# A one-core AdaLN block: x of all batches kept in SBUF, the maxima's two parts made by POOL, the first quad's parts moved SBUF to SBUF

## The chip, the cores and the metric

The kernel runs on one core of one Trainium2 chip. The metric is the time of one execution on the device in microseconds; the figure used is the median of the runs. The kernel before has a median of 712.5 us over three runs (710.43 to 712.85).

## What is computed

The block has eight batches of 512 tokens with 128 features, 16 heads of width 8. All of it is fp32 in the reference:

```
mod = (silu(c) @ wmod)                      # shifts sa, sb, scales ca, cb, gates ga, gb of each batch
h = layernorm(x) * (1 + ca) + sa
q, k, v = h @ w_qkv.T, by head              # logits = q k^T / sqrt(8)
l = logits - max(logits)
p = where(l >= 0, pos(l), 1 / (1 - l (1 - l/2 (1 - l/3))));  p /= sum(p)
x = x + ga * (p v @ w_out.T + b_out)
h = layernorm(x) * (1 + cb) + sb
x = x + gb * ffn(h)                         # 128 (and its negative) -> 512 -> 512 -> 128, weights +-1, relu
```

Since the maximum is subtracted, l is never above zero and only the reciprocal of the cubic is needed.

## The kernel before, in words

The unit of work is a group m: two blocks of 128 keys against the 512 queries of two heads, so that a tile is 128x2048 in two halves. There are 128 groups, 16 to a batch, and the program is written as steps s, one group each: batch b = s // 16, step n = s % 16. For a group, PE makes scores into the PSUM tile Z in two halves (L532), ACT squares each half with a shift (sq, L685), DVE makes the cubic from sq and Z (cub, L918, `cubic`), POOL squares the cubic (L1104, `square_of`), ACT takes the reciprocal root of that (prob, L696), and PE multiplies prob with the values (OP, L564). The ring of cubics has four places; prob of group s - 2 is made in step s.

Seven groups ahead (`AHEAD`), PE makes the logits into SA (L547) and DVE reduces them to their maxima (mx, L927, `maxima`, two of 1024 columns a step). Every fourth group, in steps 1, 5, 9 and 13, a quad is complete. Then `of_maxima` on DVE splits the negated maxima into a rounded part (L937) and the rest (L941), and transposes both into mp (L947). Eight small DMAs on SP lay mp as rows into QH (`rows_of_maxima`), where the scores' matmul subtracts the maximum as a product with rows of ones of KH. Q and K themselves are each kept as two rounded parts; `write_parts` writes them to HBM (parts_q, parts_k), `read_parts` brings a quad's rows into QL, KH and QH. This holds for the first quad too: its K parts are written and read back on ACT's queue, its Q parts on SP's.

Beside the groups run the products of the table MISC: hT, q, k, v for batch b + 1, x1 and the second norm's transposes h2T and the layer l0 for batch b - 1, layer l1 and y for batch b - 2. An entry names the step and the place (a, b, c, d) of PE's sequence in `pe_step`; ACT takes the result out of PSUM in the same step and place (`take`). They share one PSUM bank MB, so each waits until the one before was taken. FILL puts a matmul without use into steps of the batches 0 and 1.

The table AT gives the steps of the small work. For the norm of x, DVE does four bn_stats (st1, L964) and four bn_aggr (mv1, L970) in the steps 6 and 7 for batch b + 2, POOL makes the root (rs1, L1063 and L1065) and xn (L1108 to L1114) in the steps 9 and 10. x arrives by two loads a batch: xa for the norm, xb for the residual. For the norm of x1 it is st2, mv2 on DVE and rs2, x1n on POOL. POOL also keeps a copy x1k of x1 for the last sum (L1144). In the last batch (b = 7) st2 and mv2 stand at the end of step 8, after its maxima, and rs2 and x1n in step 9.

Ahead of the steps, and in the steps of batch -1, stand the set-up and the parts, logits and maxima of the first quads. The gates' rows are made by DVE (`dve_gates`). After the steps, `pe_tail` and its partners do x1, norm and feed-forward of batch 7.

## Time and profile before

| | |
|---|---|
| median of three runs | 712.5 us |
| the profiled execution, its own time | 711.12 us |
| its span in the profile | 709.3 us |
| busy share of DVE, PE, ACT, POOL | 92, 89, 83, 85% |
| mean granted clock of PE | 0.969 of full speed |

The span is what the profile covers; the execution's own time is 1.8 us longer. A busy share is a mean over the whole span, with a start of 43 us in which little is busy, seven batches that repeat, and an end with another order. So the windows of one stage and the timeline of its engines say more than the shares.

### The profile page before, as it was taken

To read this page: it belongs to the slowest core of one execution; us is meant where nothing else is said; L and a number is where in the kernel's file an instruction comes from. 1 tells how busy PE (TensorE), PEld (TensorE's weight loads), DVE (VectorE), ACT (ScalarE), POOL (GpSimd) and SP (SyncE) were. 2 spreads that over 40 slices of the span, in tenths; PEclk is the share of its full clock that TensorE was granted. 3 is DMA by queue.
4 is the path that set the end of the run, shared out by engine and by line. 5 is a ranking of instruction groups with operands and counts; after the bars stand their busy time and mean duration, and the time that the engine had idled before them with its cause. 6 is when DMAs were issued, how large, how long until landed. Compare 5 with 4: busy or idle time off the path is not lost.

```text
span 709.3 us, 9702 instructions
## 1 busy us (share of the span) xinstructions
PE 628.1 (89%) x3009; PEld 245.3 (35%) x3009; DVE 649.6 (92%) x807; ACT 587.7 (83%) x541; POOL 601.8 (85%) x414
## 2 busy tenths in 40 slices
PE   7486778777789999899989999999989999997898
PEld 5132222223222334233523343233423342334356
DVE  6989999999999999999999999999999999985843
ACT  2037788988899989998999989998999989987942
POOL 7229697898979999899989999899989998898740
PEclk9568999999999999999999999999999999998999
DMA  4524112241134114151135114331214113100100
GB/s 129 176 61 163 46 54 67 77 151 29 53 93 169 50 54 108 55 171 31 38 102 171 50 51 108 113 113 53 57 55 164 54 53 92 51 8 24 34 12 30
DMA packets 43719, 56.24 MB, mean 79 GB/s; under 512 B 11548, under 2 KB 27188, under 8 KB 43668
## 3 DMA queue, kind: packets, MB, share of 16 engines
q1 hardware_dynamic: 42606, 54.17, 25.7%
q10 hardware_dynamic: 1062, 1.45, 0.6%
q8 instruction: 24, 0.39, 0.2%
q14 instruction: 27, 0.22, 0.1%
HBM read 32.06 MB, written 18.89 MB: 72 GB/s over the span
## 4 chain that ended last, share of the span: by engine, by line
PE 45%; DVE 24%; ACT 15%; issue 13%; DMA 1%; ACTq 0%; POOL 0%; DVEq 0%; POOLq 0%
DVE cub L918 11%; DVE mx L927 10%; PE OP L564 10%; PE MB L486 9%; PE Z L532 7%; PE SA L547 7%; ACT sq L685 6%; ACT prob L696 5%; PE MB L476 2%; PE MB L499 2%; PE MB L583 1%; PE MB L454 1%; ACT hid L739 1%; DVE st L975 1%; ACT OT L747 1%
## 5 line engine op out<-in xcount | busy, mean ns | idle before, releaser
L1104 POOL TENSOR_TENSOR cub<-cub 128x2048 f32<-128x2048 f32 x128 | 460.5, 3603 | 48.3 <-DVE cub L918 48.0
L685 ACT ACTIVATE sq<-Z,shift 128x1024 f32<-128x1024 f32 x256 | 282.4, 1117 | 74.9 <-PE Z L532 73.0
L918 DVE SCALAR_TENSOR_TENSOR cub<-sq,Z 128x1024 f32<-128x1024 f32 x256 | 309.6, 1210 | 16.2 <-ACT sq L685 15.7
L927 DVE TENSOR_REDUCE mx<-SA 128x2 f32<-128x1024 f32 x248 | 301.7, 1216 | 11.0 <-PE SA L547 8.0
L696 ACT ACTIVATE prob<-cub 128x2048 f32<-128x2048 f32 x128 | 244.4, 1911 | 0.5 <-PE OP L564 0.5
L547 PE MATMUL SA<-KH,QL 64*128 64x512 f32 x496 | 121.5, 486 | 37.5 <-DVE mx L927 28.0
L532 PE MATMUL Z<-QH,KH 64*128 64x512 f32 x512 | 129.0, 500 | 17.3 <-DVE cub L918 17.0
L564 PE MATMUL OP<-prob,Vq 128*16 128x512 f32 x1024 | 135.2, 601 | 0.0
L532 PEld LDWEIGHTS Z<-QH,KH 64*128 64x128 f32 x512 | 48.3, 184 | 196.1 <-DVE cub L918 116.1
L486 PE MATMUL MB<-hid,W 128*128 128x512 f32 x192 | 108.0, 645 | 0.0
L547 PEld LDWEIGHTS SA<-KH,QL 64*128 64x128 f32 x496 | 47.3, 187 | 120.5 <-DVE mx L927 89.5
L476 PE MATMUL MB<-h2T,W 128*128 128x512 f32 x56 | 32.4, 661 | 7.0 <-ACT hid L739 4.7
L486 PEld LDWEIGHTS MB<-hid,W 128*128 128x128 f32 x192 | 28.6, 188 | 23.4 <-issue 23.4
L583 PE MATMUL MB<-W,ident 128*128 128x512 f32 x52 | 33.1, 721 | 0.6 <-ACT x L721 0.6
L564 PEld LDWEIGHTS OP<-prob,Vq 128*16 128x16 f32 x1024 | 16.9, 94 | 45.6 <-issue 40.9
L499 PE MATMUL MB<-W2G,hid 128*128 128x128 f32 x192 | 29.0, 298 | 0.7 <-ACT x L721 0.7
L499 PEld LDWEIGHTS MB<-W2G,hid 128*128 128x128 f32 x192 | 24.6, 201 | 6.4 <-issue 5.5
L454 PE MATMUL MB<-hT,wq 128*128 128x512 f32 x16 | 10.7, 754 | 7.1 <-ACT hT L707 7.1
L747 ACT ACTIVATE OT<-OP 128x512 f32<-128x512 f32 x28 | 16.5, 591 | 0.0
L739 ACT ACTIVATE hid<-MB,sv 128x512 f32<-128x512 f32 x24 | 16.3, 679 | 0.0
L1065 POOL TENSOR_TENSOR rs<-rs,half 128x4 f32<-128x4 f32 x15 | 15.2, 1017 | 1.2
L1124 POOL TENSOR_SCALAR SQ<-SQ 128x512 fp32r<-128x512 f32 x7 | 4.3, 618 | 13.9 <-ACT SQ L716 13.9
(194 smaller groups left out, 478.5 us busy)
## 6 DMA issues: line engine op xcount, KB each, us to landing
QL<-parts_q SPq DMA_DIRECT2D x64, 128.0 KB, 2.5
QH<-parts_q SPq DMA_DIRECT2D x64, 128.0 KB, 2.8
KH<-parts_k SPq DMA_DIRECT2D x62, 128.0 KB, 2.6
parts_q<-SQ SPq DMA_DIRECT2D x28, 256.0 KB, 2.5
parts_k<-SK SPq DMA_DIRECT2D x28, 256.0 KB, 2.7
QH<-mp SPq DMA_DIRECT2D x253, 2.0 KB
nd<-OT SPq DMA_DIRECT2D x124, 32.0 KB
xa<-L_attn_x SPq DMA_DIRECT2D x8, 256.0 KB, 4.0
```

The lines of the kernel that those rows point to most:

```text
L476: mm = nc.tensor.matmul(bank, W0[:, m * P:(m + 1) * P], h2T[:, :], start=True, stop=True)
L486: mm = nc.tensor.matmul(bank, W1f[:, kc, m * P:(m + 1) * P], hid0[:, kc, :], start=(kc == 0), stop=(kc == KC - 1))
L499: mm = nc.tensor.matmul(bank4[:, t, :], hid1[:, kc, t * P:(t + 1) * P], W2G[:, kc, :], start=(kc == 0), stop=(kc == KC - 1))
L532: mm = nc.tensor.matmul(Z[:, h, e * S:(e + 1) * S], KH[rows, 2 * g + r, keys], QH[rows, 2 * g + r, :], start=True, stop=True)
L547: mm = nc.tensor.matmul(unit_bank(m, u)[:, e, :], QL[rows, 2 * g + r, qt * P:(qt + 1) * P], KH[rows, 2 * g + r, :], start=True, stop=True)
L564: mm = nc.tensor.matmul(OP[32 * j:32 * j + 2 * HD, :], Vq[:, tb, hh, :, :].rearrange("p d a -> p (d a)"), slot[:, tb % 2, j % 2, :], start ...
L583: nc.tensor.matmul(MB[:, :], ident[:, :], W1f[:, n % KC, :], start=True, stop=True)
L685: nc.scalar.activation(sq[:, h, :], Z[:, h, :], ACT.Square, bias=shift[:, 0:1]).then_inc(s_sq, 1)
L696: nc.scalar.activation(prob[:, m % RING, :], cub[:, m % RING].rearrange("p a n -> p (a n)"), RSQRT)\
L918: nc.vector.scalar_tensor_tensor(cub[:, m % RING, h, :], sq[:, h, :], CUB_ADD, Z[:, h, :], ALU.add, ALU.mult).then_inc(s_cv, 1)
L927: nc.vector.tensor_reduce(to, unit_bank(m, u)[:, :, :], AX_X, ALU.max).then_inc(s_mx, 1)
L1104: nc.gpsimd.tensor_tensor(ff, ff, ff, ALU.mult).then_inc(s_fp, 1)
```

## The change

x is loaded once, in three DMAs (batch 0, batches 1 to 3, batches 4 to 7), into a tile xs of all batches. x1 and the residual are made in place in xs; xa, xb, x1 and x1k with their loads and copies are gone. The statistics of all batches are taken at the start: of batches 0 to 3 by DVE, of 4 to 7 by ACT, which sums each of 16 tiles (128x128) in an accumulating Copy (step 3 of batch -1) and, after POOL has made the means, an accumulating Square (step 6). POOL takes the roots for 12 and for 16 tiles in one `pow` each (`norms_of_x`).

DVE's reduction now gives the negated maxima at once; POOL makes the two parts (`parts_of_maxima`) at the head of the steps 1, 5, 9, 13, and DVE transposes after its second cubic of that step as before (`rows_of`). Rows of parts, of maxima and of constants lie interleaved in the partitions, so that the first quad's parts can go by DMA from SQ and SK into QL, QH and KH (`first_quad`). POOL makes the gates, and clears the later half of KH. v moves from step 13 to 11, y from 11 to 12 to 11 to 13, k from place c to d, w2g from step 8 to step 0. FILL has changed in step 12.

In the last batch the stats, the roots and x1n have other steps and DVE makes x1n; x1 stands in place b, y in a bank of its own; DVE makes the last group's square. In the tail POOL multiplies 96 of 128 rows of num, and x1's sums are split so that the part of those rows comes first.

```diff
 LOADS = 4
+ON_VECTOR = 4
+X_LOADS = (slice(0, 1), slice(1, 4), slice(4, B))
...
-    ("hT", 1, [(0, "c", 4)]), ("q", 1, [(0, "d", 4)]), ("k", 1, [(1, "c", 4)]),
+    ("hT", 1, [(0, "c", 4)]), ("q", 1, [(0, "d", 4)]), ("k", 1, [(1, "d", 4)]),
...
-    ("y", -2, [(11, "c", 1), (11, "d", 1), (12, "c", 1), (12, "d", 1)]),
-    ("v", 1, [(13, "c", 4)]), ("h2T", -1, [(13, "d", 4)]),
+    ("v", 1, [(11, "c", 4)]),
+    ("y", -2, [(11, "d", 1), (12, "c", 1), (12, "d", 1), (13, "c", 1)]), ("h2T", -1, [(13, "d", 4)]),
...
-    ("x1", -1, [(8, "a", 2), (8, "c", 2)]),
-    ("y", -2, [(8, "d", 1), (9, "c", 1), (9, "d", 1), (10, "c", 1)]),
+    ("x1", -1, [(8, "b", 2), (8, "c", 2)]),
+    ("y", -2, [(9, "b", 1), (9, "c", 1), (9, "d", 1), (10, "b", 1)]),
...
 FILL = {(FIRST, n): ("v", 1) for n in range(13, 16)}
-FILL |= {(0, n): ("k", 2) for n in range(2, 13)} | {(0, n): ("v", 2) for n in (14, 15)}
-FILL |= {(1, n): ("k", 3) for n in range(2, 8)} | {(1, n): ("x1", 1) for n in range(9, 13)}
+FILL |= {(0, n): ("k", 2) for n in range(2, 12)} | {(0, n): ("v", 2) for n in range(12, 16)}
+FILL |= {(1, n): ("k", 3) for n in range(2, 8)} | {(1, n): ("x1", 1) for n in range(9, 12)} | {(1, 12): ("v", 3)}
...
 MAIN_AT = {"xbg": 6, "wog": 5, "den_sq": 6, "den_inv": 6, "att": 7, "st2": 9, "mv2": 10, "rs2": 11, "x1n": 11,
-           "w2g": 8, "st1": 6, "mv1": 7, "rs1": 9, "xn": 10}
+           "w2g": 0, "xn": 10}
 AT = {b: MAIN_AT for b in range(FIRST, B)}
-AT[B - 1] = MAIN_AT | {"w2g": 4, "st2": 8, "mv2": 8, "rs2": 9, "x1n": 9}
+AT[B - 1] = MAIN_AT | {"st2": 9, "mv2": 9, "rs2": 9, "x1n": 10}
...
         own_bank = {product(FIRST, "k", 0): (SA[:, 0, :], None),
-                    product(B - 1, "l1_0", B - 2): (SA[:, 0, :], None), product(B - 1, "l1_1", B - 2): (SA[:, 1, :], None),
+                    product(B - 1, "y", B - 3): (SA[:, 1, :], None),
+                    product(B - 1, "l1_0", B - 2): (SA[:, 0, :], None),
+                    product(B - 1, "l1_1", B - 2): (SA[:, 1, :], product(B - 1, "y", B - 3)),
                     product(B, "l1_3", B - 2): (SA[:, 0, :], product(B - 1, "l1_0", B - 2)),
...
+        def first_quad(eng, to, name, s_done):
+
+            src, places = (SQ, PLACES_Q) if name == "q" else (SK, PLACES_K)
+            for a in range(PARTS):
+                if a == 0:
+                    eng.wait_ge(s_hi, "qk".index(name) + 1)
+                else:
+                    eng.wait_ge(s_taken[name], 1)
+                for place in places[a]:
+                    eng.dma_start(to[2 * place:P:STEP_D, 0:2, :].bitcast(F32), src[0:P // NQ, a, :].bitcast(F32))\
+                        .then_inc(s_done, 16)
...
             elif first and b == B - 1:
-                pe.wait_ge(s_mp, NQ * B)
+                pe.wait_ge(s_mx, 2 * GROUPS)
...
-            pe.wait_ge(s_att, B)
+            pe.wait_ge(t_att, 1)
             pe.wait_ge(s_wog, B)
             pe.wait_ge(s_xbg, B)
             for t in range(TB):
                 to = t_x1_banks[t // 2][:, t % 2, :]
-                nc.tensor.matmul(to, num[:, t * P:(t + 1) * P], woG[:, :], start=True, stop=False)
-                mm = nc.tensor.matmul(to, ident[:, :], xb[:, t, :], start=False, stop=True)
+                nc.tensor.matmul(to, ident[:, :], xs[:, B - 1, t, :], start=(t % 2 == 0), stop=False, skip_group_check=True)
+                nc.tensor.matmul(to, num[0:LAST, t * P:(t + 1) * P], woG[0:LAST, :], start=False, stop=False,
+                                 skip_group_check=True)
+            pe.wait_ge(s_att, B)
+            for t in range(TB):
+                to = t_x1_banks[t // 2][:, t % 2, :]
+                mm = nc.tensor.matmul(to, num[LAST:P, t * P:(t + 1) * P], woG[LAST:P, :], start=False, stop=(t % 2 == 1),
+                                      skip_group_check=True)
                 if t % 2 == 1:
                     mm.then_inc(t_x1, 1)
...
+            if b == FIRST and n in (3, 6):
+
+                act.wait_ge(s_x[2], 16)
+                if n == 6:
+                    act.wait_ge(s_mean1, 1)
+                for i in range((B - ON_VECTOR) * TB):
+                    tile = xs[:, ON_VECTOR + i // TB, i % TB, :]
+                    scratch = hid[n // 6][:, i // TB, i % TB * D:(i % TB + 1) * D]
+                    if n == 3:
+                        mm = nc.scalar.activation(scratch, tile, ACT.Copy, accum_out=sum1[:, i:i + 1])
+                    else:
+                        mm = nc.scalar.activation(scratch, tile, ACT.Square, bias=mean1[:, i:i + 1],
+                                                  accum_out=sq1[:, i:i + 1])
+                mm.then_inc(s_sum1 if n == 3 else s_sq1, 1)
             if s == 4 - AHEAD:
...
 
+        def stats_of_x(dve, beta):
+
+            own = slice(TB * beta, TB * (beta + 1))
+            for i, load in enumerate(X_LOADS):
+                if load.start <= beta < load.stop:
+                    dve.wait_ge(s_x[i], 16)
+            for t in range(TB):
+                bn = nc.vector.bn_stats(st1[:, TB * beta + t, :], xs[:, beta, t, :])
...
+        def last_square(dve):
+            dve.wait_ge(s_cv, 2 * GROUPS)
+            ff = cub[:, (GROUPS - 1) % RING].rearrange("p a n -> p (a n)")
+            nc.vector.tensor_tensor(ff, ff, ff, ALU.mult).then_inc(s_last_fp, 1)
 
         def sums_of(dve, quad):
             dve.wait_ge(s_pv, QUAD * (quad + 1))
...
-            def of_maxima(m, stage):
+                nc.vector.tensor_reduce(to, unit_bank(m, u)[:, :, :], AX_X, ALU.max, negate=True).then_inc(s_mx, 1)
...
+            def rows_of(m):
...
-                    dve.wait_ge(s_mx, 2 * m)
-                    nc.vector.tensor_reduce(mx[:, i, 1, :], mx[:, i, 0, :].bitcast(F32).rearrange("p (c a) -> p c a", a=1),
-                                            AX_X, ALU.max, negate=True).then_inc(s_mh, 1)
-                elif stage == 1:
-                    dve.wait_ge(s_mh, quad + 1)
-                    nc.vector.tensor_reduce(mx[:, i, 2, :].bitcast(F32), mx[:, i, 0:2, :].bitcast(F32).rearrange("p a c -> p c a"),
-                                            AX_X, ALU.add, negate=True).then_inc(s_ml, 1)
-                else:
-                    dve.wait_ge(s_ml, quad + 1)
-                    if quad >= 2:
-                        dve.wait_ge(s_mrow[(quad - 2) % NQ], ((quad - 2) // NQ + 1) * M_DMAS * 16)
-                    nc.vector.transpose(mp[:, i, :], mx[:, i, 1:1 + PARTS, :].rearrange("p a c -> p (a c)").bitcast(F32))\
-                        .then_inc(s_mp, 1)
+                dve.wait_ge(s_ml, quad + 1)
+                if quad >= 2:
+                    dve.wait_ge(s_mrow[(quad - 2) % NQ], ((quad - 2) // NQ + 1) * M_DMAS * 16)
+                nc.vector.transpose(mp[:, i, :], mx[:, i, 1:1 + PARTS, :].rearrange("p a c -> p (a c)").bitcast(F32))\
+                    .then_inc(s_mp, 1)
...
+            def norm_late():
+
+                norm_sums()
+                if at(s, "x1n", -1, b, n):
+                    dve.wait_ge(s_made["h2T"], B - 2)
+                    dve.wait_ge(s_rs2, B - 1)
+                    for t in range(TB):
+                        last = nc.vector.tensor_scalar(x1n[:, t, :], xs[:, b - 1, t, :], mv2[:, t, 0:1], rs2[:, t:t + 1],
+                                                       ALU.subtract, ALU.mult)
+                    last.then_inc(s_x1n, 1)
+
             m = s + AHEAD
             cubic(s, 0)
-            of_maxima(m, 0)
             maxima(m, 0)
-            of_maxima(m, 1)
             split(b, n)
+            if b == B - 1:
+                norm_late()
             cubic(s, 1)
-            of_maxima(m, 2)
+            rows_of(m)
             maxima(m, 1)
...
+            if s == GROUPS - 1:
+                last_square(dve)
...
+        def norms_of_x(pool, late):
+
+            cols = slice(ON_VECTOR * TB, B * TB) if late else slice(TB, ON_VECTOR * TB)
+            if late:
+                pool.wait_ge(s_sq1, 1)
+                nc.gpsimd.tensor_scalar(rs1[:, cols], sq1[:, :], 1.0 / D, EPS, ALU.mult, ALU.add).then_inc(s_ve1, 1)
+            else:
+                pool.wait_ge(s_mv1, ON_VECTOR)
+                nc.gpsimd.tensor_scalar(rs1[:, cols], mv1[:, TB:, 1], 1.0, EPS, ALU.mult, ALU.add).then_inc(s_ve1, 1)
+                nc.gpsimd.tensor_scalar(nm1[:, cols], mv1[:, TB:, 0], -1.0, 0.0, ALU.mult, ALU.add).then_inc(s_nm1, 1)
+            pool.wait_ge(s_ve1, 3 if late else 2)
+            nc.gpsimd.tensor_tensor(rs1[:, cols], rs1[:, cols], half[:, cols], ALU.pow).then_inc(s_rs1, 1)
+            pool.wait_ge(s_rs1, 3 if late else 2)
+            if late:
+                nc.gpsimd.tensor_tensor(nm1[:, cols], mean1[:, :], rs1[:, cols], ALU.mult).then_inc(s_nmr1, 1)
+            else:
+                pool.wait_ge(s_nm1, 1)
+                nc.gpsimd.tensor_tensor(nm1[:, cols], nm1[:, cols], rs1[:, cols], ALU.mult).then_inc(s_nmr1, 1)
...
+            def parts_of_maxima(m):
+
+                if not (0 < m <= GROUPS and m % QUAD == 0):
+                    return
+                quad = m // QUAD - 1
+                i = quad % 2
+                pool.wait_ge(s_mx, 2 * m)
+                need(pool, s_mp, quad - 1)
+                nc.gpsimd.tensor_scalar(mx[:, i, 1, :], mx[:, i, 0, :].bitcast(F32), 1.0, 0.0, ALU.mult, ALU.add).then_inc(s_mh, 1)
+                pool.wait_ge(s_mh, quad + 1)
+                nc.gpsimd.tensor_tensor(mx[:, i, 2, :], mx[:, i, 0, :].bitcast(F32), mx[:, i, 1, :].bitcast(F32), ALU.subtract)\
+                    .then_inc(s_ml, 1)
+
+            parts_of_maxima(s + AHEAD)
+            if n == 14 and 2 <= b < B - 1:
                 pool.wait_ge(s_taken["y"], b - 1)
...
-            pool.wait_ge(s_y, B - 2)
-            nc.gpsimd.tensor_scalar(x1k[:, :, :], x1[:, :, :], 1.0, 0.0, ALU.mult, ALU.add).then_inc(s_x1k, 1)
+            pool.wait_ge(t_den, 2)
+            nc.gpsimd.tensor_tensor(num[0:LAST], num[0:LAST], den[0:LAST], ALU.mult).then_inc(t_att, 1)
...
+            def load_x(i):
+                own = X_LOADS[i]
+                sp.dma_start(xs[:, own], x_t[:, own.start * TB:own.stop * TB, :].rearrange("p (b t) d -> p b t d", t=TB))\
+                    .then_inc(s_x[i], 16)
+
+            load_x(0)
             sp.dma_start(c_rows, c).then_inc(ld_c, 16)
...
                 need(sp, s_qh[NQ - 1], beta * 2 * 16)
                 if beta == 0:
-                    write_parts(sp, "q", 0, FIRST_QUAD)
+                    sp.wait_ge(s_zero, 2)
+                    first_quad(sp, QL, "q", s_qk[0])
+                    first_quad(sp, QH, "q", s_qh[0])
+                    sp.wait_ge(s_con, 2)
+                    sp.wait_ge(s_zero, 4)
+                    for e in range(2):
+                        r = ROWS * e + R_CON
+                        sp.dma_start(QH[r:r + 3:2, :, :].bitcast(F32), const_q).then_inc(s_rows, 16)
                     write_parts(sp, "q", 0, OTHER_QUADS)
                 else:
                     write_parts(sp, "q", beta)
                     write_parts(sp, "k", beta)
```

**DVE, batch 2, around a quad's end** (step 5 and the start of 6). Before; L918 is the cubic, L927 the maxima, L937 and L941 the two parts, L947 the transpose, L964 the stats of x for batch 4:

```order
L918 SCALAR_TENSOR_TENSOR cub<-sq,Z 128x1024
L937 TENSOR_REDUCE mx<-mx 128x16
L927 TENSOR_REDUCE mx<-SA 128x2
L941 TENSOR_REDUCE mx<-mx 128x16
L918 SCALAR_TENSOR_TENSOR cub<-sq,Z 128x1024
L947 STREAM_TRANSPOSE mp<-mx 128x32
L927 TENSOR_REDUCE mx<-SA 128x2
L918 SCALAR_TENSOR_TENSOR cub<-sq,Z 128x1024
L927 TENSOR_REDUCE mx<-SA 128x2
L918 SCALAR_TENSOR_TENSOR cub<-sq,Z 128x1024
L927 TENSOR_REDUCE mx<-SA 128x2
L964 BN_STATS st<-xa 128x6 x4
```

Now (L966 is the cubic, L975 the maxima, L986 the transpose):

```order
L975 TENSOR_REDUCE mx<-SA 128x2
L966 SCALAR_TENSOR_TENSOR cub<-sq,Z 128x1024
L986 STREAM_TRANSPOSE mp<-mx 128x32
L975 TENSOR_REDUCE mx<-SA 128x2
L966 SCALAR_TENSOR_TENSOR cub<-sq,Z 128x1024
L975 TENSOR_REDUCE mx<-SA 128x2
L966 SCALAR_TENSOR_TENSOR cub<-sq,Z 128x1024
L975 TENSOR_REDUCE mx<-SA 128x2
L966 SCALAR_TENSOR_TENSOR cub<-sq,Z 128x1024
L975 TENSOR_REDUCE mx<-SA 128x2
L966 SCALAR_TENSOR_TENSOR cub<-sq,Z 128x1024
```

The two parts between the cubics and the stats are gone from DVE; the transpose has stayed in its place.

**POOL, from the set-up to the first square.** Before; L1094 makes W1, L1063 and L1065 the root for batch 1, L1114 its xn:

```order
L1094 TENSOR_SCALAR W<-prob 128x2048
L1095 TENSOR_SCALAR W<-prob 128x512
L1063 TENSOR_TENSOR rs<-mv,eps 128x4
L1065 TENSOR_TENSOR rs<-rs,half 128x4
L1108 TENSOR_TENSOR nm<-mv,rs 128x4
L1110 TENSOR_SCALAR nm<-nm 128x4
L1114 TENSOR_SCALAR xn<-xa,rs,nm 128x128 x4
L1136 COPY Vq<-Vn 128x4x32 x2
L1104 TENSOR_TENSOR cub<-cub 128x2048
```

Now, behind eight operations of the gates; L1153 is the `pow` for 12 and then 16 tiles, L1195 xn of batch 1, L1240 and L1242 the first quad's two parts:

```order
L1150 TENSOR_SCALAR rs<-mv 128x12
L1151 TENSOR_SCALAR nm<-mv 128x12
L1153 TENSOR_TENSOR rs<-rs,half 128x12
L1159 TENSOR_TENSOR nm<-nm,rs 128x12
L1163 TENSOR_SCALAR mean<-sum 128x16
L1195 TENSOR_SCALAR xn<-xs,rs,nm 128x128 x4
L1147 TENSOR_SCALAR rs<-sq 128x16
L1153 TENSOR_TENSOR rs<-rs,half 128x16
L1156 TENSOR_TENSOR nm<-mean,rs 128x16
L1240 TENSOR_SCALAR mx<-mx 128x16
L1242 TENSOR_TENSOR mx<-mx 128x16
L1230 COPY Vq<-Vn 128x4x32 x2
```

The norms of all batches now stand ahead of the first quad's parts, which POOL makes.

**DVE, batch 7, steps 8 and 9.** Before; L975 and L981 are the statistics of x1 of batch 6, L890 copies the sums of a quad:

```order
L927 TENSOR_REDUCE mx<-SA 128x2
L975 BN_STATS st<-x 128x6 x4
L981 BN_AGGR mv<-st 128x2 x4
L890 COPY OT<-OP 128x512
L918 SCALAR_TENSOR_TENSOR cub<-sq,Z 128x1024
L937 TENSOR_REDUCE mx<-mx 128x16
L941 TENSOR_REDUCE mx<-mx 128x16
L918 SCALAR_TENSOR_TENSOR cub<-sq,Z 128x1024
L947 STREAM_TRANSPOSE mp<-mx 128x32
```

Now (L1003, L1009 the statistics, L1019 x1n, L938 the copy):

```order
L975 TENSOR_REDUCE mx<-SA 128x2
L938 COPY OT<-OP 128x512
L966 SCALAR_TENSOR_TENSOR cub<-sq,Z 128x1024
L1003 BN_STATS st<-xs 128x6 x4
L1009 BN_AGGR mv<-st 128x2 x4
L966 SCALAR_TENSOR_TENSOR cub<-sq,Z 128x1024
L986 STREAM_TRANSPOSE mp<-mx 128x32
L966 SCALAR_TENSOR_TENSOR cub<-sq,Z 128x1024
L1019 TENSOR_SCALAR x1n<-xs,mv,rs 128x128 x4
L966 SCALAR_TENSOR_TENSOR cub<-sq,Z 128x1024 x3
```

The statistics have moved behind the first cubic of step 9, and x1n has come to DVE, between the cubics of step 10.

## Rows read from the trace of the kernel before

**Rows 1.** Page, part 1: busy us, share of the span, instructions.
```profile
PE 628.1 (89%) x3009; PEld 245.3 (35%) x3009; DVE 649.6 (92%) x807; ACT 587.7 (83%) x541; POOL 601.8 (85%) x414
```

**Rows 2.** Windows: length, busy us (instructions) by engine, PEclk, DMA, GB/s.
```profile
282.00:360.35 78.35, 74.40 (x364) 27.93 (x364) 76.62 (x93) 73.81 (x70) 75.13 (x53) 1.00 0.29 89
...
633.97:665.57 31.60, 23.93 (x130) 11.53 (x128) 20.41 (x32) 23.74 (x21) 23.38 (x15) 0.89 0.08 20
...
665.57:709.30 43.73, 40.76 (x224) 25.10 (x224) 21.43 (x37) 19.70 (x21) 17.30 (x21) 1.00 0.10 26
```

**Rows 3.** Timeline of DVE, batch 3, steps 5 and 6: start, us, line.
```profile
306.08 0.16 DVE L937 TENSOR_REDUCE mx<-mx 128x16 fp32r<-128x16 f32 x1
...
307.43 0.18 DVE L941 TENSOR_REDUCE mx<-mx 128x16 f32<-128x32 f32 x1
...
308.65 0.20 DVE L947 STREAM_TRANSPOSE mp<-mx 128x32 f32<-128x32 f32 x1
...
314.42 0.86 DVE L964 BATCH_NORM_STATS2 st<-xa 128x6 f32<-128x128 f32 x4
```

**Rows 4.** Windows: batch 6, from its first cubic to that of batch 7.
```profile
515.54:593.31 77.77, 74.27 (x365) 27.93 (x366) 75.74 (x84) 73.69 (x70) 72.46 (x45) 1.00 0.28 85
```

**Rows 5.** Windows: batch 3's steps 13 to 15.
```profile
345.10:360.35 15.25, 14.38 (x77) 5.98 (x76) 14.60 (x17) 15.25 (x17) 15.25 (x8) 1.00 0.38 104
```

**Rows 6.** Timeline of POOL in batch 3.
```profile
290.06 0.62 POOL L1124 TENSOR_SCALAR SQ<-SQ 128x512 fp32r<-128x512 f32 x1 [2.08 <-ACT SQ L716]
...
301.30 7.17 POOL L1104 TENSOR_TENSOR cub<-cub 128x2048 f32<-128x2048 f32 x2
...
342.25 7.16 POOL L1104 TENSOR_TENSOR cub<-cub 128x2048 f32<-128x2048 f32 x2
```

**Rows 7.** POOL groups: count, busy us, mean ns, idle before.
```profile
L1168 POOL TENSOR_TENSOR W2G<-W,gB 128x128 f32<-128x128 f32 x28 | 12.0, 467 | 0.0
...
L1065 POOL TENSOR_TENSOR rs<-rs,half 128x4 f32<-128x4 f32 x15 | 15.2, 1017 | 1.2
...
L1193 POOL TENSOR_TENSOR rs<-rs,half 128x2 f32<-128x2 f32 x2 | 1.4, 699 | 0.2
...
L1110 POOL TENSOR_SCALAR nm<-nm 128x4 f32<-128x4 f32 x14 | 2.8, 202 | 1.2
```

**Rows 8.** Timeline of the start.
```profile
14.30 1.50 ACTq L392 DMA_DIRECT2D parts_k<-SK  x2
...
24.74 0.80 PE L547 MATMUL SA<-KH,QL 64*128 64x512 f32 x2 [9.49 <-DMA KH<-parts_k]
...
36.18 0.21 DVE L947 STREAM_TRANSPOSE mp<-mx 128x32 f32<-128x32 f32 x1
...
43.33 1.21 DVE L918 SCALAR_TENSOR_TENSOR cub<-sq,Z 128x1024 f32<-128x1024 f32 x1
```

**Rows 9.** DMA issues: count, KB each, us to landing.
```profile
parts_k<-SK ACTq DMA_DIRECT2D x4, 64.0 KB, 2.5
```

**Rows 10.** Groups of ACT's instructions, two sizes with immediate scale.
```profile
L747 ACT ACTIVATE OT<-OP 128x512 f32<-128x512 f32 x28 | 16.5, 591 | 0.0
...
L696 ACT ACTIVATE prob<-cub 128x2048 f32<-128x2048 f32 x128 | 244.4, 1911 | 0.5 <-PE OP L564 0.5
```

**Rows 11.** Timeline of the start, POOL beside DVE.
```profile
15.05 1.90 POOL L1094 TENSOR_SCALAR W<-prob 128x2048 fp32r<-128x2048 uint8 x1
...
15.34 1.75 DVE L862 TENSOR_SCALAR prob<-prob 8x256 f32<-8x256 f32 x1
```

**Rows 12.** Timeline of DVE in batch 7, end of step 8.
```profile
633.97 1.21 DVE L918 SCALAR_TENSOR_TENSOR cub<-sq,Z 128x1024 f32<-128x1024 f32 x1
...
636.73 1.23 DVE L927 TENSOR_REDUCE mx<-SA 128x2 f32<-128x1024 f32 x1 [1.55 <-PE SA L547]
...
639.85 0.87 DVE L975 BATCH_NORM_STATS2 st<-x 128x6 f32<-128x128 f32 x4 [1.89 <-ACT x L721]
...
641.63 1.21 DVE L918 SCALAR_TENSOR_TENSOR cub<-sq,Z 128x1024 f32<-128x1024 f32 x1
```

273 lines of the change are left out of this document (132 added, 141 removed).

## The prediction

> **What bounds the kernel now.** I read the page's busy shares first, then the windows of one repeated batch and of the end, then the timelines of DVE, ACT and POOL in them. The shares [rows 1] name DVE, with 92%. The window of batch 3 says more [rows 2]: in 78.35 us DVE is busy for 76.62, POOL for 75.13, PE for 74.40 and ACT for 73.81. So DVE sets the pace, but each of the others has only 3.2 to 4.5 us of room in a batch: no edit to DVE alone can bring more than that. The reader is to see two more things. In the steps 13 to 15 ACT is busy for all of 15.25 us [rows 5]; there ACT sets the pace, not DVE. And in the end the two windows differ: from 634 to 665.6 us no engine is full (PE 23.9 of 31.6, ACT 23.7), while from there to 709.3 PE is busy for 40.8 of 43.7 [rows 2]. What comes earlier in the first of them moves the whole end forward.
>
> **Part 1, the repeated batches.** DVE loses, per quad, L937 and L941. They take 0.16 and 0.18 us [rows 3], of which a part lies beside their neighbours: some 0.3 us, 1.2 a batch. It also loses the statistics of x (four stats in 0.86 us, L964 [rows 3], and four aggregates). What these are worth is shown by the kernel itself: batch 6 has none, since there is no batch 8, and takes 77.77 us [rows 4] against 78.35 [rows 2]. So about 0.6 us a batch, though more than 0.86 is left out: the rest is taken back by ACT and PE.
>
> POOL gets the two parts. The nearest row is L1110, 128x4 in 0.20 us [rows 7]; two of them with the wait between are about 0.5 us. It loses per batch the root of x (0.2 + 1.02), two small products (0.4) [rows 7] and the copy x1k, and gains four times 0.5: its sum stays about as it is. What counts is when the parts are ready, since behind DVE's transpose stand a reduction and the next cubics. POOL makes them after the square of the step before. In step 5 that square ends at 301.30 + 7.17 = 308.5 us, in a stretch in which POOL runs without a gap from 290.06, where it waited for ACT's SQ [rows 6]; parts at 309.0 against a transpose that stood at 308.65 [rows 3] and would now want to start at 308.1. DVE then waits 0.9 us and the gain of steps 1 and 5 becomes a loss of 0.3. In step 13 the square ends at 342.25 + 7.16 = 349.4 [rows 6], but w2g (four of 0.467, less overlap 1.7 us [rows 7]), the root and the small products are gone from the steps before it, so I put the wait at 0.5 us. In the steps 1 and 9 I see none. v moved to step 11 takes 0.5 us of ACT from the full stretch to one with room.
>
> The batch then changes by +0.3 (to step 5), -0.8 (statistics, steps 6 and 7), -0.3 (step 9), and -0.5 (steps 13 to 2, where ACT's load is what falls): -1.3. As no neighbour gives all of its room back, I take **-1.1**, for the batches 0 to 5, -0.5 for batch 6 and -0.3 for the half of batch 7 with maxima: -7.4 us. The bounds: only the statistics count, and a wait eats the rest (-0.4 a batch, -3.2), or no wait at all (-1.9 a batch, -13). The x loads and x1k were off the path; they are costed at nothing, covered by a DMA share of 0.29 [rows 2].
>
> **Part 2, the start.** Before, K of the first quad goes out from 14.30 us, and the first logits wait for its way through HBM until 24.74; the transpose of the first quad stands at 36.18, the first cubic at 43.33 [rows 8]. Four DMAs on ACT's queue at 1.50 / 2 = 0.75 us each [rows 8] and a landing of 2.5 [rows 9] would bring K by 14.3 + 3.0 + 2.5 = 19.8: the logits come 5 us sooner. But the first quad's parts are now POOL's, behind the norms of all batches. POOL: set-up to 19.3 (W1 starts at 15.05 [rows 11] and is put back by a memset of KH, estimated 1.8; W1 and W2 take 2.5), then eight dependent operations of the gates, which I put at 0.5 us each with their waits, to 23.4; the `pow` for 12 tiles. A `pow` takes 0.70 us for 2 and 1.02 for 4 columns [rows 7], so 0.38 + 0.16 n: 2.3 us for 12, 2.9 for 16. With its neighbours the early norms end at 26.5. ACT's first 16 sums are done by then, its 16 squares follow: a Copy costs (1911 - 591) / 1536 = 0.86 ns a column and 0.15 us beside [rows 10], so 0.26 us for 128, 0.2 back to back; a Square with a bias pointer perhaps 0.3. That is 4.8 us, to 31.5; then the late norms, 3.5 us, to 35.0, and the parts, to 35.5. The transpose then stands at 35.7 and not at 36.18: **the 5 us shrink to about 0.4**, and I take -0.3. The bounds: no wait for POOL at all (-5); each accumulating operation at twice my price, 0.5 and 0.6 us, with the sums 3 and the squares 5 us longer (+4 where a part is covered).
>
> **Part 3, batch 7 and the tail.** After cubic 633.97 of step 8 the next cubic starts at 641.63 [rows 12], 7.7 us on where 2.3 to 2.5 is usual: x1 stands ahead of the logits on PE, DVE's last maxima wait for it (1.55 us), then DVE waits for x1 itself (1.89), then come its statistics and a copy [rows 12]. Now the logits stand ahead of x1, and the cubic of step 9 ahead of the statistics: it can start at about 637. That is 4.6 us; POOL's root and DVE's x1n come behind, and y no longer holds the bank that h2T needs. Against it: DVE's x1n reads SBUF with one tensor input. In the start DVE's L862 did the same beside POOL's L1094: started at 15.34 with 256 columns, it took 1.75 us and ended at 17.09, just after L1094's end at 16.95, where its size alone asks for some 0.4 [rows 11]. So x1n may wait for POOL's square, which takes 7.17 / 2 = 3.6 us [rows 6]; up to 2.5 us of it in step 10. I take -4.5 from the order and +1 from the block; the last square on DVE brings a part of 1.4 us, since PE is full there (-0.5), and the four more matmuls of x1's sums cost 0.4 on PE. Sum -3.6, between 0 and -7.
>
> On x1n the Trainium skill speaks against the change: "SBUF — State Buffer", section "Who interferes with whom", says that GpSimd's port pair is VectorE's second, that a one-source operation with both sides in SBUF can take it, and that whichever of the two issues second fully blocks for the other's whole instruction. By it x1n could stand for a whole square, 3.6 us instead of my 1, and the sum would be 2.6 us less of a gain. The row of the start agrees as far as it goes.
>
> **The sum.** -7.4 - 0.3 - 3.6 = -11.3 us. From the profiled execution's own 711.12 us that gives 699.8; as that execution lies 1.4 us under the median of 712.5, I predict **700.5 us**, 1.7% less.
>
> **The rivals.**
> - *The neighbours take it back.* ACT and PE are so full that a batch gains 0.4 us and the end 2: 711.1 - 3.2 - 0.3 - 2 = 705.6. For it speaks batch 6, against it DVE's 76.62 of 78.35 us [rows 2]. 0.18.
> - *No waits for POOL.* The chip runs POOL's parts ahead of the transposes and batch 7 gives its full 7: 711.1 - 13 - 1 - 6.5 = 690.6. For it speaks that a wait in one quad lets POOL catch up for the next. 0.12.
> - *The start is lost to ACT's sums.* An accumulating operation costs twice my price: the transpose of the first quad at 40, all else as forecast: 704. 0.07.
> - *It doesn't do what it says:* the stall of batch 7 stays in another form (x1n behind POOL's square, twice) and waits cancel part 1: 710. 0.05.
> - *Slower: DVE waits for POOL in every quad.* There are 31 transposes behind POOL. If the wait is 1.2 us in each, as it would be where POOL stays a step behind after x1n (3.6 us of work in step 11), 37 us come on, less what the slack of 1 us a step takes back: 711.1 + 37 - 11 - 20 = 717. It decides from about 0.9 us a quad. Against it: POOL sat idle 2.08 us in step 1 [rows 6]. 0.04.
>
> My forecast has 0.54. A measurement of this kernel can tell about 0.5% (3.6 us) from no change. Faster by over that is 0.54 + 0.18 + 0.12 + 0.07 less some tails: 0.86; the same 0.09; slower 0.05. The range is 691 to 707.5: it takes in the rivals on the faster side but for their ends.
>
> **What would show it.** Right: a batch of about 77.2 us; DVE's transposes of the steps 5 and 13 waiting for POOL, those of 1 and 9 not; first logits near 20 us but the first cubic near 43; the gap after the last maxima down from 7.7 to 3 us. Wrong: batches of 78 us with DVE waiting for ACT; a first cubic near 38 or at 47; x1n operations of 2 us and more.

## The result: 0.7% slower, not faster

The changed kernel takes 717.16 us (median of 5 runs, 715.46 to 717.52), the kernel before 710.84 (median of 5, 710.43 to 712.85). The ratio is 1.007, with a 95% interval of 1.0049 to 1.0091. I had forecast 700.5 us in a range of 691 to 707.5, and the chance of 0.05 for slower was the one that came.

The profiled execution has a span of 715.2 us where that of before has 709.3. The page's busy line, to be held against [rows 1]:

```profile
PE 629.7 (88%) x3019; PEld 244.3 (34%) x3019; DVE 640.4 (90%) x704; ACT 599.7 (84%) x606; POOL 611.1 (85%) x454
```

DVE is freed of 9 us of work (649.6 to 640.4), POOL and ACT are loaded with 9 and 12 more, and the span is longer. So the question is where the 9 us of DVE went. I cut both spans at the first cubic of each batch, which gives the account that all the rest hangs on (us; the last group's first cubic divides the last two):

| stretch | before | after | difference | my forecast |
|---|---|---|---|---|
| start to the first cubic | 43.33 | 45.62 | +2.29 | -0.3 |
| batch 0 | 79.81 | 81.45 | +1.64 | -1.1 |
| batch 1 | 78.99 | 81.77 | +2.78 | -1.1 |
| batches 2 to 5, each | 78.35 | 78.39 | +0.04 | -1.1 |
| batch 6 | 77.77 | 78.38 | +0.61 | -0.5 |
| batch 7 to the last group | 75.93 | 72.26 | -3.67 | } -3.9 |
| from the last group to the end | 40.04 | 42.21 | +2.17 | } |
| sum | 709.29 | 715.25 | +5.96 | -11.3 |

So the forecast missed by 17.3 us: 6.6 of them lie in the batches 0 and 1, 5.7 in the batches 2 to 6, 2.6 in the start and 2.4 in batch 7 and the tail.

**A repeated batch.** The windows of batch 3, of its steps 13 to 15 and of batch 6 answer to [rows 2], [rows 5] and [rows 4], with the same columns:

```profile
287.22:365.62 78.40, 74.41 (x365) 27.86 (x366) 75.29 (x78) 73.96 (x70) 74.69 (x56) 1.00 0.26 81
350.63:365.62 14.99, 14.10 (x83) 6.60 (x82) 14.03 (x15) 14.53 (x15) 14.21 (x10) 1.00 0.27 77
522.39:600.77 78.38, 74.43 (x365) 27.84 (x366) 75.26 (x77) 73.95 (x70) 73.00 (x52) 1.00 0.27 81
```

DVE is busy for 75.29 us instead of 76.62, and the batch is as long as it was. I cut batch 3 into steps too, each from its first cubic to the next step's. Step 6, where the statistics stood, became 0.80 us shorter and step 9 0.10; step 5 became 0.31 longer, step 7 0.17, and the steps 13 and 14 together 0.40 (0.71 longer and 0.31 shorter). DVE's timeline says what stands there: the cubic behind the transpose of step 1, the transpose of step 5, and the first maxima and the transpose of step 13, to be held against [rows 3]. The number in brackets is the wait ahead of the instruction, and for whom:

```profile
297.74 1.22 DVE L966 SCALAR_TENSOR_TENSOR cub<-sq,Z 128x1024 f32<-128x1024 f32 x1 [0.64 <-ACT sq L720]
...
315.69 0.21 DVE L986 STREAM_TRANSPOSE mp<-mx 128x32 f32<-128x32 f32 x1 [0.34 <-POOL mx L1242]
...
352.25 1.23 DVE L975 TENSOR_REDUCE mx<-SA 128x2 f32<-128x1024 f32 x1 [0.41 <-PE SA L576]
...
355.05 0.21 DVE L986 STREAM_TRANSPOSE mp<-mx 128x32 f32<-128x32 f32 x1 [0.45 <-POOL mx L1242]
```

In the steps 5 and 13 DVE waits 0.34 and 0.45 us for POOL's second part; in the steps 1 and 9 it doesn't, and in the batches 0 and 1 no transpose waits for more than 0.1 us. In step 1 DVE waits 0.64 us for ACT's square (sq), just as the kernel before did: there DVE's two reductions had stood in time that DVE spent waiting anyway.

**The start**, to be held against [rows 8]:

```profile
17.69 0.79 PE L576 MATMUL SA<-KH,QL 64*128 64x512 f32 x2 [3.88 <-DMA KH<-SK]
...
27.93 0.20 POOL L1163 TENSOR_SCALAR mean<-sum 128x16 f32<-128x16 f32 x1
...
28.23 0.40 ACT L817 ACTIVATE hid<-xs,mean 128x128 f32<-128x128 f32 x1 [5.04 <-POOL mean L1163]
...
34.01 0.39 ACT L817 ACTIVATE hid<-xs,mean 128x128 f32<-128x128 f32 x1
...
34.58 0.20 POOL L1147 TENSOR_SCALAR rs<-sq 128x16 f32<-128x16 f32 x1 [4.72 <-ACT hid L817]
34.87 2.90 POOL L1153 TENSOR_TENSOR rs<-rs,half 128x16 f32<-128x16 f32 x1
...
38.44 0.22 POOL L1242 TENSOR_TENSOR mx<-mx 128x16 fp32r<-128x16 f32 x1
...
38.69 0.21 DVE L986 STREAM_TRANSPOSE mp<-mx 128x32 f32<-128x32 f32 x1 [6.79 <-POOL mx L1242]
...
45.62 1.21 DVE L966 SCALAR_TENSOR_TENSOR cub<-sq,Z 128x1024 f32<-128x1024 f32 x1
```

The logits start at 17.69 us, 7 us sooner than before. The first transpose stands at 38.69, 2.5 us later than before, since it waits 6.79 us for POOL. POOL waited 4.72 us for ACT's sums of squares, and ACT 5.04 us for POOL's means.

**Batch 1, steps 6 and 7**, first of the kernel before, then of the changed one:

```profile
152.34:157.66 5.32, 3.75 (x22) 1.10 (x18) 5.32 (x9) 3.92 (x3) 5.32 (x6) 1.00 0.08 18
157.66:162.90 5.24, 3.65 (x22) 1.13 (x18) 4.88 (x10) 5.07 (x5) 5.09 (x3) 1.00 0.53 150
```

```profile
156.76:161.30 4.54, 2.92 (x10) 0.97 (x6) 4.54 (x5) 3.92 (x3) 4.54 (x6) 0.77 0.08 17
161.30:168.88 7.58, 6.08 (x31) 1.55 (x30) 4.70 (x6) 5.10 (x6) 5.86 (x3) 0.91 0.34 104
```

The column behind POOL's is PE's granted clock: 1.00 before, 0.77 and 0.91 now. In PE's timeline the matmul without use (L612) takes 2.07 us at 159.90 and 1.13 at 165.70, so the clock was at its lower level of 1.2 GHz in between, for about 3.4 us if the two shares are worked out: (0.23 x 4.54 + 0.09 x 7.58) / 0.5. The two steps together take 12.12 us, where before they took 10.56.

The clock decides much of the batches 0, 1 and 7, and nothing of the others: in all fourteen profiles of this study the mean granted clock of each of the batches 2 to 6 is 1.00.

**Batch 1, step 3**, is 0.47 us longer than before. PE's matmul without use of step 2, before and now:

```profile
135.95 1.13 PE L583 MATMUL MB<-W,ident 128*128 128x512 f32 x2
```

```profile
140.37 1.12 PE L612 MATMUL MB<-W,ident 128*128 128x512 f32 x2 [0.40 <-ACT SK L754]
```

It waits until ACT has taken k out of the shared bank. k now stands in place d of step 1, behind PE's logits and not ahead of them, and ACT takes it out behind prob and not ahead of it. The wait of 0.40 us puts PE's next products and scores back; it stands in the traces of all thirteen kernels that have k in its new place.

**Batch 7 and the tail.** DVE from the end of step 8 to step 10 (before: [rows 12]), then DVE, POOL and PE behind the last group's cubic:

```profile
641.40 1.21 DVE L966 SCALAR_TENSOR_TENSOR cub<-sq,Z 128x1024 f32<-128x1024 f32 x1
...
644.26 1.21 DVE L966 SCALAR_TENSOR_TENSOR cub<-sq,Z 128x1024 f32<-128x1024 f32 x1
...
650.24 3.15 DVE L1019 TENSOR_SCALAR x1n<-xs,mv,rs 128x128 f32<-128x128 f32 x4
653.31 2.34 DVE L966 SCALAR_TENSOR_TENSOR cub<-sq,Z 128x1024 f32<-128x1024 f32 x2
...
675.20 3.75 POOL L1271 TENSOR_TENSOR W2G<-W,gB 128x128 f32<-128x128 f32 x4
675.71 2.52 DVE L933 TENSOR_TENSOR cub<-cub 128x2048 f32<-128x2048 f32 x1
...
678.15 0.68 DVE L948 TENSOR_SCALAR QL<-MB 128x512 fp32r<-128x512 f32 x1
...
679.61 0.50 PE L518 MATMUL SA<-QL,W 128*128 128x512 f32 x1 [1.27 <-DVE QL L950]
...
690.49 0.38 PE L646 MATMUL Z<-xs,ident 128*128 128x128 f32 x2
...
692.36 1.15 PE L652 MATMUL Z<-woG,nd 32*128 32x128 f32 x8
...
693.45 0.82 PE L528 MATMUL SA<-W2G,hid 128*128 128x128 f32 x5
```

The 7.7 us between two cubics are 2.9 now (641.40 to 644.26). But x1n takes 3.15 us on DVE beside POOL's square, the last square stands on DVE ahead of the split of QL (678.15) for which PE waits 1.27 us, and x1's sums take PE from 690.49 to 693.45. The windows of the steps 8 and 9 and of the steps 10 to 12, before and now:

```profile
631.70:644.58 12.88, 9.45 (x56) 4.57 (x54) 9.18 (x18) 8.94 (x8) 9.67 (x10) 1.00 0.03 8
644.58:661.85 17.27, 13.72 (x68) 6.82 (x66) 9.82 (x11) 13.99 (x12) 13.91 (x5) 0.80 0.07 20
```

```profile
639.12:649.10 9.98, 9.37 (x56) 4.58 (x54) 8.82 (x16) 8.84 (x8) 8.33 (x7) 1.00 0.04 10
649.10:665.64 16.54, 12.16 (x68) 5.30 (x66) 12.62 (x15) 13.54 (x12) 14.07 (x4) 0.90 0.08 23
```

The steps 8 and 9 gave 2.9 us. The other 0.7 came in steps whose granted clock differs, 0.80 and 0.90.

### The profile page after: what moved, and what is told of

The parts are those of the page before. It is cut to its first block, busy times and chain, and to the rows that moved or that the text cites. A ratio compares the mean times of both kernels' runs of the same rounds, so it can differ in the third digit from the quotient of the medians.

```text
span 715.2 us, 9709 instructions
## 1 busy us (share of the span) xinstructions
PE 629.7 (88%) x3019; PEld 244.3 (34%) x3019; DVE 640.4 (90%) x704; ACT 599.7 (84%) x606; POOL 611.1 (85%) x454
## 4 chain that ended last, share of the span: by engine, by line
POOL 38%; PE 26%; DVE 15%; issue 11%; ACT 8%; SPq 1%; DMA 0%; POOLq 0%; ACTq 0%; DVEq 0%
POOL cub L1190 26%; DVE cub L966 8%; DVE mx L975 6%; PE OP L593 5%; PE Z L561 4%; PE SA L576 3%; PE MB L515 3%; ACT prob L734 3%; PE MB L505 3%; ACT sq L720 3%; PE MB L612 1%; POOL x1n L1195 1%; POOL xn L1195 1%; POOL xs L1262 1%; POOL SK L1221 1%
## 5 line engine op out<-in xcount | busy, mean ns | idle before, releaser
L966 DVE SCALAR_TENSOR_TENSOR cub<-sq,Z 128x1024 f32<-128x1024 f32 x256 | 309.8, 1212 | 12.2 <-ACT sq L720 12.1
L975 DVE TENSOR_REDUCE mx<-SA 128x2 f32<-128x1024 f32 x248 | 302.1, 1218 | 20.1 <-PE SA L576 15.1
L593 PE MATMUL OP<-prob,Vq 128*16 128x512 f32 x1024 | 137.1, 609 | 0.0
L612 PE MATMUL MB<-W,ident 128*128 128x512 f32 x54 | 35.4, 742 | 1.0 <-ACT xs L757 0.6
L528 PE MATMUL MB<-W2G,hid 128*128 128x128 f32 x160 | 23.2, 288 | 1.3 <-ACT Vn L765 1.3
L528 PEld LDWEIGHTS MB<-W2G,hid 128*128 128x128 f32 x160 | 19.4, 191 | 6.5 <-issue 3.7
L986 DVE STREAM_TRANSPOSE mp<-mx 128x32 f32<-128x32 f32 x32 | 6.6, 207 | 10.7 <-POOL mx L1242 10.6
L775 ACT ACTIVATE hid<-MB 128x512 f32<-128x512 f32 x24 | 14.2, 592 | 0.0
```

The costliest lines, as they stand in the source:

```text
L528: mm = nc.tensor.matmul(bank4[:, t, :], hid1[:, kc, t * P:(t + 1) * P], W2G[:, kc, :], start=(kc == 0), stop=(kc == KC - 1))
L593: mm = nc.tensor.matmul(OP[32 * j:32 * j + 2 * HD, :], Vq[:, tb, hh, :, :].rearrange("p d a -> p (d a)"), slot[:, tb % 2, j % 2, :], start ...
L612: nc.tensor.matmul(MB[:, :], ident[:, :], W1f[:, n % KC, :], start=True, stop=True)
L966: nc.vector.scalar_tensor_tensor(cub[:, m % RING, h, :], sq[:, h, :], CUB_ADD, Z[:, h, :], ALU.add, ALU.mult).then_inc(s_cv, 1)
L975: nc.vector.tensor_reduce(to, unit_bank(m, u)[:, :, :], AX_X, ALU.max, negate=True).then_inc(s_mx, 1)
```

## The experiments

Twelve kernels. a1 to a4, b1 to b3, d1 and d2 are the changed kernel with one edit (b3 with two, in different stretches); c1 to c3 put edits together. Since single runs of one kernel of this program spread by up to some 10 us, the reading of each is the stretch of its profile that its edit touches, and the median stands beside it. In the last column the kernels that leave the tail alone scatter between 41.68 and 42.21; the four with 41.7 (a2, a3, b1, d1) have a low clock in the steps 13 or 14 of batch 7, just ahead of it (so has b2, with 42.06). All ratios are to the kernel before, with their 95% interval.

| kernel | median us | ratio | first cubic | batch 1 | batch 3 | last group to end |
|---|---|---|---|---|---|---|
| changed | 717.16 | 1.007 [1.0049, 1.0091] | 45.62 | 81.77 | 78.40 | 42.21 |
| a1, parts on DVE | 708.11 | 0.9954 [0.9932, 0.9977] | 39.23 | 81.85 | 78.01 | 42.20 |
| a2, late norms behind the first quad | 709.26 | 0.9971 [0.995, 0.9991] | 39.52 | 81.74 | 78.38 | 41.69 |
| a3, no fill in step 12 | 718.48 | 1.0107 [1.0071, 1.0142] | 46.11 | 82.45 | 78.37 | 41.69 |
| a4, last square on POOL | 719.17 | 1.0109 [1.0074, 1.0145] | 46.48 | 83.57 | 78.35 | 40.78 |
| b1, v and y of before | 720.50 | 1.0113 [1.0086, 1.014] | 46.77 | 85.18 | 78.37 | 41.69 |
| b2, two fills | 718.60 | 1.0084 [1.0053, 1.0114] | 46.06 | 87.77 | 78.35 | 42.06 |
| b3, x1n on POOL, sums whole | 716.38 | 1.0079 [1.0047, 1.011] | 46.05 | 81.73 | 78.35 | 40.92 |
| c1, a1 + a4 + b3 + b2 | 707.60 | 0.9936 [0.9911, 0.9961] | 39.75 | 85.30 | 78.02 | 40.11 |
| c2, a1 + a4 + b3 | 707.82 | 0.9938 [0.9915, 0.9961] | 39.56 | 81.87 | 77.99 | 40.07 |
| c3, a1 + a4 + b3 + b1 | 701.88 | 0.9888 [0.9838, 0.9938] | 39.49 | 79.44 | 77.80 | 39.73 |
| d1, statistics in batch 1 | 718.15 | 1.0102 [1.0063, 1.0141] | 46.24 | 82.79 | 78.39 | 41.68 |
| d2, transpose later | 715.16 | 1.0056 [1.0028, 1.0083] | 45.78 | 85.26 | 77.95 | 42.20 |

### a1: the two parts on DVE again

```diff
+                if stage == 0:
+                    nc.vector.tensor_reduce(mx[:, i, 1, :], mx[:, i, 0, :].bitcast(F32).rearrange("p (c a) -> p c a", a=1),
+                                            AX_X, ALU.max, negate=True).then_inc(s_mh, 1)
...
+                if stage == 1:
+                    nc.vector.tensor_reduce(mx[:, i, 2, :].bitcast(F32), mx[:, i, 0:2, :].bitcast(F32).rearrange("p a c -> p c a"),
+                                            AX_X, ALU.add, negate=True).then_inc(s_ml, 1)
...
             cubic(s, 0)
+            rows_of(m, 0)
             maxima(m, 0)
+            rows_of(m, 1)
...
-            parts_of_maxima(s + AHEAD)
```

> The changed kernel with the maxima's two parts made by DVE again, in the places of before. Theory (POOL's parts cost what the statistics gave): the transposes of steps 5 and 13 no longer wait for POOL, so step 5 loses 0.3 us and the steps 13 and 14 together 0.4; batches 2 to 6 take 77.7 to 77.8 us instead of 78.4, and the first quad's transpose stands 6 us earlier since it no longer waits behind the norms. In all 711 to 708 us against 717.2. Rival (v's and y's new places cost the step 13, not POOL): the steps 13 and 14 keep their 10.2 us, a batch takes 78.1 and more. Rival 2 (DVE is still what bounds): the two reductions put 0.3 us back into each quad and the batch stays at 78.4.

The batches are 78.0 us, 0.39 less than the changed kernel's but more than the 77.7 to 77.8 expected, and the first cubic stands at 39.23, 6.4 us earlier. Step 5 falls from 5.23 to 4.89, as said. The steps 13 and 14 fall only from 10.17 to 10.04, where I expected 9.8; c3 shows what holds the rest. DVE in step 13:

```profile
342.58 0.16 DVE L985 TENSOR_REDUCE mx<-mx 128x16 fp32r<-128x16 f32 x1
...
344.20 0.18 DVE L990 TENSOR_REDUCE mx<-mx 128x16 f32<-128x32 f32 x1
...
345.43 0.20 DVE L996 STREAM_TRANSPOSE mp<-mx 128x32 f32<-128x32 f32 x1
```

The transpose waits for nobody. Rival 2 falls: with both reductions back on DVE the batch is shorter. And they hardly cost DVE anything: the cubic behind L990 starts 0.10 us after it, though it takes 0.18.

### a2: the first quad ahead of the late norms

```diff
-            if b == FIRST and n == 12:
+            if b == FIRST and n == 13:
                 norms_of_x(pool, True)
```

> The changed kernel with one edit: POOL makes the late norms of x (batches 4 to 7) in step 13 of batch -1, behind the first quad's parts instead of ahead of them. Theory (the start waits for POOL, POOL for ACT's sums): the first transpose stands at about 32 us instead of 38.7, the first cubic at 39 to 40 instead of 45.6, the total at 711. Rival (the start is bound by the second quad's loads, which wait on SP behind the gates' row): the first cubic moves by less than 3 us. Rival 2 (the clock of PE eats it): the cubic comes at 39, but the batches 0 and 1 grow by what the start gave.

The median is 7.9 us lower. In the profile 6.1 us of it lie before the first cubic, and 2.3 in batch 0 (79.14 and not 81.45), which has fewer stretches at the lower clock. The timeline:

```profile
30.44 0.22 POOL L1242 TENSOR_TENSOR mx<-mx 128x16 fp32r<-128x16 f32 x1
...
31.06 1.23 DVE L975 TENSOR_REDUCE mx<-Z 128x2 f32<-128x1024 f32 x1 [4.15 <-PE Z L576]
...
32.20 0.20 DVE L986 STREAM_TRANSPOSE mp<-mx 128x32 f32<-128x32 f32 x1
...
34.91 0.20 POOL L1147 TENSOR_SCALAR rs<-sq 128x16 f32<-128x16 f32 x1 [4.25 <-ACT hid L817]
```

POOL's parts are done at 30.7 us; the transpose at 32.20 then stands behind maxima that waited 4.15 us for PE (loads of the second quad), so of the first rival a small part is true. POOL still waits 4.25 us for ACT's squares, but nobody waits for POOL now. This settles the start.

### a3: no matmul without use in step 12

```diff
-FILL |= {(0, n): ("k", 2) for n in range(2, 12)} | {(0, n): ("v", 2) for n in range(12, 16)}
-FILL |= {(1, n): ("k", 3) for n in range(2, 8)} | {(1, n): ("x1", 1) for n in range(9, 12)} | {(1, 12): ("v", 3)}
+FILL |= {(0, n): ("k", 2) for n in range(2, 12)} | {(0, n): ("v", 2) for n in (14, 15)}
+FILL |= {(1, n): ("k", 3) for n in range(2, 8)} | {(1, n): ("x1", 1) for n in range(9, 12)}
```

> The changed kernel without the matmul without use in step 12 of the batches 0 and 1 and in step 13 of batch 0. Theory (the fill right behind v's product holds the logits back): step 12 of both batches falls from 5.8 to about 4.8 us, 2 us in all, 715. Rival (the fill keeps PE's clock up): the granted clock drops somewhere in the batches 0 and 1 and the time stays or rises. It should also show whether the fall of the clock in step 6 of batch 1 comes again.

My theory falls. Step 12 keeps 5.81 us in batch 0 and 5.77 in batch 1, and right behind it the clock goes down and the next steps are longer: steps 13 and 14 of batch 1 take 10.32 us instead of 9.85.

```profile
190.76:196.53 5.77, 4.47 (x30) 1.95 (x26) 4.63 (x5) 4.66 (x5) 5.77 (x6) 1.00 0.06 15
196.53:201.15 4.62, 3.21 (x14) 0.74 (x14) 4.62 (x7) 4.24 (x4) 4.28 (x4) 0.77 0.09 21
```

The fall in step 6 of batch 1 came again (0.76).

### a4: the last square on POOL

```diff
-                if 0 <= m < GROUPS - 1:
+                if 0 <= m < GROUPS:
...
-            if s == GROUPS - 1:
-                last_square(dve)
```

> The changed kernel with the last group's square on POOL again. Theory (the square on DVE, 2.5 us, stands ahead of the split that PE waits for): PE's wait of 1.27 us for the split goes, the time from the last group's first cubic to the end falls from 42.2 to 41.1 us; 716.1. Rival (PE is full there in any case): no change. Rival 2 (POOL's 3.6 us for it is later than DVE's 2.5): up to 1 us longer.

From the last group's first cubic to the end it is 40.78 us instead of 42.21: 1.4 us, where I expected 1.1. But this profile has the low clock in the steps 13 and 14 of batch 7, and four kernels with that and the tail untouched have 41.7; against them it is 0.9 us. So the edit is worth 0.9 to 1.4. DVE's split now stands at 683.61, 2.5 us behind that cubic instead of 5.1, and POOL's W2G takes 1.71 us instead of 3.75:

```profile
683.61 0.68 DVE L945 TENSOR_SCALAR QL<-MB 128x512 fp32r<-128x512 f32 x1
...
687.33 1.71 POOL L1266 TENSOR_TENSOR W2G<-W,gB 128x128 f32<-128x128 f32 x4
```

The median is 719.2 us all the same, since the batches 0 and 1 took 85.07 and 83.57 us in that profile (81.45 and 81.77 in the changed kernel's). The edit stands in the last step and cannot have done that: the same instructions met another clock, with more stretches at the lower level. What an edit of 1 us is worth can't be read from this program's total, only from its stretch.

### b1: v and y in the steps of before

```diff
-    ("v", 1, [(11, "c", 4)]),
-    ("y", -2, [(11, "d", 1), (12, "c", 1), (12, "d", 1), (13, "c", 1)]), ("h2T", -1, [(13, "d", 4)]),
+    ("y", -2, [(11, "c", 1), (11, "d", 1), (12, "c", 1), (12, "d", 1)]),
+    ("v", 1, [(13, "c", 4)]), ("h2T", -1, [(13, "d", 4)]),
...
-            if n == 14 and 2 <= b < B - 1:
+            if n == 13 and 2 <= b < B - 1:
```

> The changed kernel with v, y (with POOL's sum of it) and the matmuls without use in the steps of before. The parts stay with POOL. Theory (step 12 of the batches 0 and 1 grew by 1.0 to 1.3 us because v's product stands there, not because of the fill): those two steps fall to 4.5 and 4.8 us; in the batches 2 to 6 the steps 12 to 14 take 14.5 to 14.6 us instead of 14.9, if v's place is what cost 0.4 there, or keep 14.9, if it is POOL's parts. Rival: v in step 13 meets the wait for POOL and step 13 takes 5.8 us, the batch 78.6.

Step 12 falls to 4.53 us in both batches. As taking the matmul without use away had left it at 5.8 (a3), v's product in the place ahead of it was the cause there. In batch 3 the steps 12 to 14 take 14.90 us, as with the change, though PE's logits now come sooner. DVE's maxima, which waited 0.41 us for them in step 13, wait 0.14 now; its transpose waits for POOL so much the longer, 0.69 us and not 0.45:

```profile
359.10 0.21 DVE L986 STREAM_TRANSPOSE mp<-mx 128x32 f32<-128x32 f32 x1 [0.69 <-POOL mx L1242]
```

The median gained nothing: in batch 1 the clock fell in the steps 4 and 5 and from 8 to 11, with 8.28 us in step 9.

```profile
174.12:182.40 8.28, 8.28 (x42) 4.47 (x38) 5.49 (x11) 5.00 (x5) 4.87 (x4) 0.76 0.05 12
```

### b2: two matmuls without use in the steps 4 to 6 of batch 1

```diff
-                    nc.tensor.matmul(MB[:, :], ident[:, :], W1f[:, n % KC, :], start=True, stop=True)
+                    for _ in range(2 if b == 1 and n in (4, 5, 6) else 1):
+                        nc.tensor.matmul(MB[:, :], ident[:, :], W1f[:, n % KC, :], start=True, stop=True)
```

> The changed kernel with two matmuls without use instead of one in the steps 4, 5 and 6 of batch 1. Theory (the granted clock falls to half in step 6 of batch 1, since with the statistics gone PE and DVE go through the steps 6 and 7 otherwise; more work of PE keeps it up): the windows of steps 6 and 7 show a clock of 1.00 and step 7 takes 5.3 us instead of 7.6; batch 1 is 79.5 us instead of 81.8. Rival (the clock falls for another reason): it falls all the same, and the steps grow by 0.5 each. Rival 2: it falls some steps later instead, and the batch stays near 81.8.

Rival 2 comes nearest: the clock falls some steps later. But the batch is longer than that says. The clock was 1.00 in the steps 4 to 7; step 5 grew by 0.85 us, step 6 by 0.36, and step 7 shrank by 1.0. Then the clock fell in the steps 8 and 9, and again in 14 and 15, where the changed kernel's profile has no fall. The steps 9 and 15:

```profile
176.60:184.54 7.94, 7.94 (x34) 4.82 (x32) 5.61 (x11) 5.11 (x5) 5.67 (x4) 0.62 0.05 11
209.52:217.84 8.32, 8.32 (x26) 2.40 (x22) 4.70 (x5) 5.22 (x5) 4.75 (x3) 0.56 0.38 111
```

Batch 1 takes 87.8 us, 6 more. How much of that the edit did isn't shown. The fall in the steps 14 and 15, which makes step 15 3.5 us longer, also stands in d2's profile, with 8.34 us in step 15, and a smaller one in d1's, and neither has doubled matmuls. In the step with the lowest clock PE is busy for all of it (8.32 of 8.32 us at 0.56).

### b3: x1n of batch 7 on POOL, and x1's sums whole

```diff
-AT[B - 1] = MAIN_AT | {"st2": 9, "mv2": 9, "rs2": 9, "x1n": 10}
+AT[B - 1] = MAIN_AT | {"st2": 9, "mv2": 9, "rs2": 9, "x1n": 9}
...
-            if at(s, "x1n", -1, b, n) and b < B - 1:
+            if at(s, "x1n", -1, b, n):
                 normalise_x1(b - 1)
...
-                nc.tensor.matmul(to, num[0:LAST, t * P:(t + 1) * P], woG[0:LAST, :], start=False, stop=False,
-                                 skip_group_check=True)
...
-                mm = nc.tensor.matmul(to, num[LAST:P, t * P:(t + 1) * P], woG[LAST:P, :], start=False, stop=(t % 2 == 1),
-                                      skip_group_check=True)
+                nc.tensor.matmul(to, num[:, t * P:(t + 1) * P], woG[:, :], start=True, stop=False)
+                mm = nc.tensor.matmul(to, ident[:, :], xs[:, B - 1, t, :], start=False, stop=True)
```

> The changed kernel with x1n of batch 7 on POOL in step 9, and with the tail's sums of x1 over all 128 rows at once, as before. Theory for the sums (eight more matmuls on a full PE cost 0.14 us each): from the first of x1's matmuls to the first of the last y's stand 2.0 us instead of 3.0, and the time from the last cubic to the end falls by 1.0. Theory for x1n (DVE's four operations of 3.15 us are POOL's square that they wait for): the two cubics behind them in step 10 come 1 us sooner, steps 9 to 12 of batch 7 take 20 us instead of 21.4. Rival for x1n: POOL's 1.75 us delay its own square and so prob, and the steps 9 to 12 stay at 21.4. Rival for the sums: PE waits there for num, and splitting them hid that: no change.

x1's sums take PE from 689.91 to 691.76, 1.85 us instead of 2.96; PE waits 0.24 us for num (nd), so the split had hidden a quarter of a microsecond and cost 1.1:

```profile
689.91 0.46 PE L647 MATMUL Z<-woG,nd 128*128 128x128 f32 x2 [0.24 <-DVE nd L1051]
...
691.76 2.84 PE L528 MATMUL SA<-W2G,hid 128*128 128x128 f32 x24
```

The steps 10 and 11 take 9.71 us instead of 10.64: 0.9 us for x1n, which takes POOL 1.74 us where it had taken DVE 3.15. The tail is 1.3 us shorter than the changed kernel's, and 0.8 shorter than in the four profiles that share its low clock in step 13. Both theories held; of the 2.1 us that the steps 9 to 12 lost, 1.1 are the clock in step 12 (5.90 us in the changed kernel, 4.76 here), which the edit may or may not have moved.

### c1 and c2: the pieces together

c1 has the edits of a1, a4, b3 and b2; c2 the same without b2's.

> The changed kernel with the parts on DVE in every quad, the last square and x1n on POOL, x1's sums whole, and two matmuls without use in steps 4 to 6 of batch 1. Theory (the pieces add up): start 39.2 us, batch 1 at 79.6, batches of 78.0, the end 3 us shorter than the changed kernel's: 702 us, faster than both kernels. Rival (they hide each other; PE is the bound at the end in any case): 706.

> The changed kernel with the parts on DVE, the last square and x1n on POOL and x1's sums whole, and with the single matmuls without use of the change. Theory (the pieces add up, the doubled matmuls cost batch 1 3.4 us of the clock): first cubic at 39.2 to 39.8, batch 1 at 81.8, batches of 78.0, the span about 702.5, the time 704. Rival (the clock falls of itself in that batch, whatever fills it): batch 1 stays at 85 and the time at 707.5.

In c1 the forecast of 702 us was missed (707.60), mostly by batch 1: it takes 85.3 us, with the clock low in the steps 4, 5, 8 and 9. In c2's profile it takes 81.87, and the span is 702.3 us, as expected. But that is the fastest of ten runs, with a mean clock of 0.973; the other nine lie at 706.9 to 709.0 us with 0.964 to 0.969, and the median is 707.82, which is what the rival said. So neither the medians nor one profile of each tell c1 from c2, and what the doubled matmuls cost stays open. The pieces themselves add up: the first cubic, the repeated batches and the end of both (3 us shorter than the changed kernel's) are as forecast, and the tail of c2 is the kernel before's (40.07 and 40.04). Both are faster than the kernel before.

### c3: v and y as well

> The kernel of c2_no_double_fills with v, y and the matmuls without use in the steps of before as well. Theory (without POOL's parts, the steps 12 to 14 lose the last 0.25 us): the batches 2 to 6 take 77.8 us, as batch 6 of the kernel before did with 77.77, and the steps 12 of the batches 0 and 1 are 1 us shorter: 2.5 to 3 us less than c2_no_double_fills, 701.5. Rival (the clock): dips of the granted clock in batch 1, as in b1_v_y_before, take back 3 us and it is no faster.

The median is 701.88 us (699.04 to 709.28), the ratio to the kernel before 0.9888: the fastest of this study. Its interval ends at 0.9938, where c2's median lies. The repeated batch is 77.8 us:

```profile
275.01:352.81 77.80, 74.30 (x365) 27.94 (x366) 75.79 (x84) 73.69 (x70) 73.09 (x48) 1.00 0.28 83
147.47:152.01 4.54, 2.97 (x18) 0.80 (x14) 4.54 (x5) 3.92 (x3) 4.54 (x6) 1.00 0.08 17
152.01:158.03 6.02, 4.77 (x26) 1.43 (x22) 4.61 (x5) 5.10 (x6) 5.43 (x3) 1.00 0.45 131
```

Step 13 falls from 5.20 us (a1) to 4.95, and 13 and 14 together are at 9.78; DVE's first maxima of step 13 wait 0.31 us for PE's logits in c2 and 0.07 here. So v's and y's new places do cost 0.25 us a batch, which b1 could not show: there POOL's parts held step 13 anyway. The two stalls lay over each other. Of the 5.0 us between the profiled spans of c2 and c3, 1.3 are the batches 2 to 6, 1.0 is step 12 of batch 0 and as much that of batch 1, and 1.6 are the fall of the clock that c2 has in batch 1 and c3 hasn't. In batch 1 the clock stays at 1.00 in the profiled run, and still the steps 6 and 7 take 10.56 us together, as in the kernel before with its statistics (5.32 + 5.24). There the statistics were worth nothing; ACT has 5.10 of 6.02 us in step 7 and POOL is full in step 6. Three of the six runs have a lower mean clock and take 704 to 709 us, as the rival on the clock has it; in which batch their clock fell isn't known, since they weren't profiled.

### d1: statistics without use in batch 1

```diff
+            if b == 1 and n in (6, 7):
+                for t in range(TB if n == 6 else 2):
+                    nc.vector.bn_stats(st1[:, TB * 3 + t, :], xs[:, 3, t, :])
```

> The changed kernel with statistics without use on DVE in batch 1: four in step 6 and two in step 7. Nothing reads them. Theory (what keeps the clock up in before is the slower pace of the steps 6 and 7, in which PE's pauses fall otherwise): step 6 takes 5.3 us, the windows of the steps 6 and 7 show a clock of 1.00, step 7 takes 5.3 us and batch 1 80.3 instead of 81.8. Rival (the clock falls for what came before step 6): it falls in step 6 or 7 all the same, and the batch is 0.5 us longer than 81.8.

The steps 6 and 7 take 5.31 and 5.23 us, to 0.01 what they took in the kernel before; but the clock falls all the same, later in step 7 (0.72), and once more in the steps 14 and 15, and batch 1 takes 82.8. So the pace of these two steps alone doesn't keep the clock up. The theory falls.

### d2: the transpose one place later

```diff
             cubic(s, 1)
-            rows_of(m)
             maxima(m, 1)
+            rows_of(m)
```

> The changed kernel with DVE's transpose of the maxima's parts one place later, behind the second maxima of its step. POOL still makes the parts. Theory (DVE waits for POOL's parts, and that wait is what the batches 2 to 6 lose): the transposes of the steps 5 and 13 wait no more, step 5 takes 4.9 us instead of 5.2, the steps 13 and 14 together 9.8 instead of 10.15, the batch 77.7 to 77.9. Rival (POOL itself is the bound there, 75 us of work in 78.4): the batch stays at 78.4, with the wait somewhere else. Rival 2 (the rows come too late for the next quad): scores wait for DMA, and the batch grows.

The batches 3 to 6 take 77.91 to 77.97 us, 0.45 less than the changed kernel's, with POOL still making the parts. No transpose behind the first waits. Step 5 takes 4.85; the steps 13 and 14 together take 10.03 and not 9.8, since v's and y's new places still hold step 13. This names the wait as the cause, and not POOL's load. (Its batch 1 took 85.3 us, by a fall of the clock in the steps 14 and 15, and batch 2 78.25, with the 0.3 us in its first step, right behind that fall.) A reader who wants POOL's parts has to give POOL one reduction more of time.

## Why the prediction was wrong, point by point

**The repeated batches, -7.4: wrong, and this is the step that carried the forecast.** Its four terms against batch 3: +0.3 for step 5 measured +0.31; -0.8 for the statistics in the steps 6 and 7 measured -0.63; -0.3 for step 9 measured -0.10; -0.5 for the steps 13 to 2 measured +0.42. That is 0.00 in place of -1.3.

The failed step is what DVE was to gain by giving up L937 and L941. "Some 0.3 us, 1.2 a batch" took the durations as the cost. The traces show how little they cost. In the kernel before, the maxima behind L937 start 1.22 us after the cubic in step 1, where 1.13 is usual; in the steps 5 and 9 it is 1.33 and 1.36, but there the changed kernel, without a reduction, has 1.30 and 1.36, since its maxima wait for PE's logits. L941 of 0.18 us costs about 0.1, and in step 1 both stand in the wait of 0.64 us for ACT. So step 5 came out right by two errors that cancel: I took a gain of 0.3 each in the steps 1 and 5 and a wait of 0.9, and measured were next to no gain and a wait of 0.34. That is luck. The wait of 0.5 us in step 13 was right (0.45).

The other failed term is "-0.5 (steps 13 to 2, where ACT's load is what falls)". [rows 5] has ACT busy for all of 15.25 us, and POOL, the last of the engines in the row, for all of 15.25 too. I read only the first. Taking work from ACT could bring nothing while POOL was as full, and to POOL went the parts. The new places of v and y also cost 0.25 us (c2 against c3) instead of giving 0.5.

POOL's parts cost 0.4 us a batch (a1 and d2 agree) while v and y stand in their new places. In that order the sum is 0.63 for the statistics, less 0.4, less 0.25: nothing is left, which is what the windows show. The two costs aren't independent: with v and y back and the parts on POOL (b1) the batch is as long as ever, so there the parts alone eat all 0.6.

**The batches 0 and 1: no term at all.** I gave them the same 1.1 us as the others. They lost 4.4. Of the 2.8 of batch 1, 1.6 are the clock in the steps 6 and 7 (c3, without the fall, has 10.56 us there and the changed kernel 12.12), some 0.8 v's place in the steps 12 to 15, and 0.47 k's in step 3. Of batch 0's 1.6, 1.3 are step 12; the rest is the clock, which fell elsewhere than before (+1.4 us in step 10, -1.4 in the steps 4 to 6). The two batches have no y and no l1, their clock does fall, and the chain of step 12 is another. A change in the table's places had to be costed for them apart. That the matmuls without use were moved along with v, and wait for k and v, should have pointed there.

**The start, -0.3: the mechanism right, the size off by 2.6.** The logits came at 17.69 (I had about 20), and the gain was eaten by POOL, as forecast: gates to 24.9 (I had 23.4), the `pow` 2.29 and 2.90 us (2.3 and 2.9). Two terms were mis-sized, and their sum is the 3 us by which the transpose stands at 38.69 and not at 35.7. The eight operations of the gates take 0.69 us each on POOL and not 0.5, so that ACT gets the means at 28.1 and not at 26.5. And each of ACT's 16 squares takes 0.385 us of pace ((34.01 - 28.23) / 15) and not 0.3. The price of POOL's order is 6.1 to 6.4 us (a2, a1); without it the start gains 3.8 to 4.1 us on the kernel before, near my bound of -5.

**Batch 7 and the tail, -3.6: measured -1.5.** The order was put at -4.5, the shrinking of one gap from 7.7 us. The gap did shrink, by 4.8 us. But the kernel before had made up for part of it in the very next step: its step 9 takes 2.95 us and the changed kernel's 4.85, so the two steps give 2.9 and not 4.5. x1n took 3.15 us beside POOL's square and cost 0.9 (b3), close to my 1. By the Trainium skill's "SBUF — State Buffer", section "Who interferes with whom", the second of the two to issue fully blocks: the trace agrees in kind. POOL's square ran from 648.93 to 652.53; the first of x1n's four operations issued at 650.24 and lasted 2.38 us, the other three 0.33 to 0.34 each, and four of this size took 1.10 us in the start of the kernel before. It happened the other way too: POOL's W2G took 3.75 us instead of 1.71 beside DVE's square, which has two SBUF inputs. How much of the rest of batch 7 is the order and how much the clock (0.80 and 0.90 in the steps 10 to 12) isn't shown; step 12 alone is 1.1 us shorter where its clock doesn't fall (4.76 in a1, b3 and d2, 5.90 in the changed kernel).

In the tail the last square was put at -0.5 and cost about 1: PE comes to x1's sums 17.45 us behind the last group's cubic, in the kernel before 16.42 and in c2 16.51. I looked at when the square would end and not at the split of QL behind it on DVE. The split sums were put at +0.4 and measure +1.1 (b3), the eight more matmuls taking 0.14 each. The two together are all of the tail's 2.2 us, as c2's tail shows.

**The last figure.** The sum gave 699.8 for an execution that lay 1.4 us under the median, so the forecast of the median should have read 701.2 and not 700.5. Either lies in the range that I gave.

**The rivals.** The one that ends slower, "DVE waits for POOL in every quad", gave 717 us, as measured, but for a false reason: it needed 1.2 us in each quad, and DVE waited 0.34 and 0.45 in two of four. The number is a coincidence; it was made by the start, by the batches 0 and 1 with their clock, and by the tail. "The neighbours take it back" is the nearest to what the repeated batches did, with POOL as the neighbour.

**What stays open.** Why the granted clock falls in step 6 of batch 1 in each of the eight profiles with v's new place and no edit in the steps 2 to 8 of that batch (the changed kernel, a1 to a4, b3, c2, d2), and not in the one of before. Less work behind it (a3), more work ahead (b2), and the old pace (d1) left the fall where it was or moved it, and did not take it away. With v and y back it fell elsewhere in b1 and nowhere in batch 1 of c3's profiled run, so v's and y's places are the first suspects; two profiles don't settle it. That k's new place makes step 3 of batch 1 0.47 us longer is read from the wait in the traces; no run has put k back.

## What to carry to other kernels

Take the price of a small instruction on the busiest engine from the difference of its neighbours' starts, not from its duration, and count it only where that engine isn't waiting for another one anyway. When a window shows one engine full, look whether a second one is full too. When work is handed to a second engine, ask what that engine has queued ahead of it at the one moment when it counts: here one call moved behind the first quad's parts was worth 6 us of the start, and one reduction between POOL's part and DVE's transpose 0.45 us a batch. Stalls that lie over each other have to be undone together: v's place cost 0 beside POOL's parts and 0.25 us a batch without them. And the shrinking of one gap is not yet a gain: see what the steps behind it took before.

## What the runs showed of the hardware

**PE's granted clock makes the spread of this program.** The six runs of c3, one kernel, in us with their mean granted clock: 699.04, 699.19 and 699.32 at 0.976; 704.44 and 706.46 at 0.964; 709.28 at 0.952. The falls are short: about 3.4 us at 1.2 GHz in batch 1 cost 1.6 us in two steps. Adding matmuls in three steps of that batch (b2) didn't keep the clock up through it: it was 0.62 in step 9 and 0.56 in step 15, of which the second fall also stands in a profile without them (d2). In the batches 2 to 6 the clock is 1.00 in all fourteen profiles.

**DVE and POOL blocked each other both ways**: x1n's four operations took 3.15 us on DVE beside POOL's square, four of the same size 1.10 in the start; W2G took 3.75 us on POOL beside DVE's square, 1.71 without it.

**An accumulating ACT operation costs a second instruction.** In the changed kernel's trace each of them is followed by an ACTIVATION_READ_ACCUMULATOR of 0.18 to 0.19 us, part of which overlaps. From start to start it is 0.29 us for a 128x128 Copy and 0.385 for a Square with a bias from a tile.
